# Two row tiles of 64 rows for the attention scores and their maxima, on alternate half steps

## Chip, cores and metric

The program runs on one core of one Trainium2 chip. The metric is the device time of one execution in microseconds. Three timed runs of the kernel before gave 635.09 us as their median (633.9 to 636.69).

## What is computed

Two transformer layers over x of shape 4 x 256 x 512, each with attention and feed-forward side by side on the same layer norm. All matrix products are in float32.

```
xn = layernorm(x)
x  = x + attn0(xn) + (gelu(xn @ W1 + b1) @ W2 + b2)             # W1: 512 x 2048
xn = layernorm(x)
x  = x + attn1(xn) + ((silu(g) * u) @ w3.T + b3), g|u = xn @ w12.T + b12
attn: 32 query heads, 8 key/value heads, head size 16, 256 tokens
      softmax(q @ k.T * scale) @ v, then an output projection
attn1 also has rotary positions and a causal mask
```

## The kernel before

**Precision.** A float32 operand is kept as a rounded part and a remainder, and a product of two operands is three products of parts. In the large projections these are three matmuls (`three`, the helper of line 693). For the scores the three products are stacked in the contraction instead: 16 head dimensions in four groups of rows of `q_sb` and `k_sb` (high, low, high, low; 64 rows), 32 rows of zeros up to `ROWS = 96`, and row 96 (`MROW`), which holds minus the row maxima in `q_sb` and ones in `k_sb`.

**Units.** There are 8 (layer, batch entry) pairs `n`, and each is worked in 4 units of 8 query heads, so 32 units `u` (`LU = 16` per layer). A unit has these steps, each with its own line on TensorE:

- `("m", u, i)`, i = 0 to 7, line 748: query-major scores of two heads, two matmuls of 256 keys (128 where the causal mask allows no more) into one PSUM bank, and in layer 1 a third one, line 753, that adds the causal mask from a bf16 tile. VectorE (line 1067) reduces the bank to minus the maximum of each row.
- `("mt", u)`, line 761: those 16 columns of maxima are transposed, and `mrow` sends them by DMA to row 96 of `q_sb`.
- `("st", u, i)`, i = 0 to 7, lines 778 and 781: key-major scores with the maxima already subtracted through row 96, one matmul of 512 columns (256 where masked) into bank 0 or 1. ScalarE (line 917) takes the exponential into `probs`; in layer 1 GpSimd (line 649) clears the upper triangle.
- `("pv", u, t)`, t = 0, 1, line 800: probabilities times values. Four matmuls stand in four column groups of 32 of the array (each is two instructions, float32 in two passes); then `norm` on VectorE and `ctx` on ScalarE and GpSimd.

**Order.** All engines walk one list, `program_order()`. `unit_slots(u)` makes 8 slots. Slot i has `st` of unit u and one `m` of unit u + 1 (i < 4) or u + 2. `spread` fills each slot with steps of the projections (`up`, `down`, `qkv`, `wo`, in parts of three or six matmuls, line 693) by the table `COST`. `with_followers` appends what drains them: `add` (VectorE, line 1105) one slot after a `down`, `hidden` (ScalarE, lines 936 and 937) right behind `up`. `work_banks` deals the banks `WORK_BANKS = (2, 3, 4, 5, 7)` to everything but `st` and `pv`, the least recently used free one first; the `m` steps take their turn there.

**Waits of `st` and `m`.** `st` number k waits for the exponential k - 2 (two banks in turn). `m` waits for whoever had its bank. The queries of a unit come over `q_parts` in DRAM by two DMAs (line 556), keys over `k_parts` (line 565) into one `k_sb`, whose halves are refilled once the last unit that reads them is through. GpSimd zeroes the spare rows at the start (lines 604 to 612).

## Time and profile before

| | |
|---|---|
| median of 3 runs | 635.09 us |
| the profiled execution | 634.52 us, its span 632.8 us |
| TensorE matmuls (PE) | 586.8 us busy, 93% of the span, 3360 instructions |
| TensorE weight loads (PEld) | 452.0 us, 71%, beside the matmuls |
| VectorE (DVE) | 438.4 us, 69% |
| ScalarE (ACT) | 356.3 us, 56% |
| GpSimd (POOL) | 213.8 us, 34% |
| granted TensorE clock, mean | 0.985 of full speed |

A matmul's record begins with its stream (or with its weight load, where that is not hidden) and ends when a model says that the result is out, so records of back-to-back matmuls overlap. What a matmul costs in a dense stretch is the distance between two starts. Where a row has several matmuls, its length is the distance from the first to the last start and the length of one.

### The profile page before, as it was taken

What the parts mean: (1) busy time and instruction counts of PE and PEld (TensorE: products, weight loads), DVE (VectorE), ACT (ScalarE), POOL (GpSimd) and SP (SyncE); (2) the same over time, 40 slices, a digit from 0 to 9 for tenths busy, and PEclk for the clock granted to TensorE, in tenths of its full rate; (3) what the DMA queues carried; (4) which work ended last, traced back from release to release, by engine and by line L of the source; (5) the groups of instructions that cost most, each with busy time, mean ns of one, the idle gap of its engine ahead of it and who ended that gap; (6) DMA issues with size and microseconds to landing.
All of it is one profiled execution on the core that took longest, in us unless ns stands there. A gap on an engine that the chain in (4) does not pass through costs nothing.

```text
span 632.8 us, 10359 instructions
## 1 busy us (share of the span) xinstructions
PE 586.8 (93%) x3360; PEld 452.0 (71%) x3360; DVE 438.4 (69%) x815; ACT 356.3 (56%) x611; POOL 213.8 (34%) x332
## 2 busy tenths in 40 slices
PE   3788899999999999999999999897999999899985
PEld 2677677787777787677877767666777877667754
DVE  6559967656566576486897685867796887487552
ACT  2337766754564683666585564655655564474440
POOL 5703423122303331111322122443643455254231
PEclk9989999999999999999999999999899999999989
DMA  5574541353233334324543323244433353344001
GB/s 187 173 207 151 134 118 67 102 150 101 69 82 103 99 101 118 84 67 134 151 134 100 85 68 117 84 105 114 127 92 102 84 142 110 85 121 116 2 17 51
DMA packets 29805, 67.30 MB, mean 106 GB/s; under 512 B 4788, under 2 KB 17588, under 8 KB 27704
## 3 DMA queue, kind: packets, MB, share of 16 engines
q1 hardware_dynamic: 21112, 38.32, 22.2%
q0 software_dynamic: 8640, 28.32, 15.2%
q8 instruction: 28, 0.46, 0.3%
q14 instruction: 25, 0.20, 0.1%
HBM read 51.67 MB, written 14.68 MB: 105 GB/s over the span
## 4 chain that ended last, share of the span: by engine, by line
PE 74%; ACT 6%; DVE 6%; DMA 5%; issue 5%; POOL 2%; SPq 1%; ACTq 0%; DVEq 0%; POOLq 0%
PE banks L693 48%; PE banks L748 8%; PE banks L800 7%; PE banks L778 7%; PE banks L753 2%; DMA q_sb<-q_parts 2%; DMA raw<-in_attn 1%; PE banks L781 1%; PE banks L713 1%; ACT L917 1%; ACT probs L917 1%; ACT hid_f L937 1%; ACT L936 1%; POOL probs L649 1%; DMA q_sb<-max_t 1%
## 5 line engine op out<-in xcount | busy, mean ns | idle before, releaser
L1067 DVE TENSOR_REDUCE neg_max<-banks 128x2 f32<-128x512 f32 (+1 forms) x256 | 158.1, 620 | 150.4 <-PE banks L748 93.7
L917 ACT ACTIVATE probs<-banks 128x512 f32<-128x512 f32 (+1 forms) x256 | 137.8, 545 | 193.8 <-PE banks L778 145.6
L693 PE MATMUL banks<-xnT,w_up 128*128 128x512 f32 x576 | 157.4, 407 | 5.4 <-issue 3.7
L693 PE MATMUL banks<-w_down,hid 128*128 128x512 f32 x480 | 129.4, 403 | 4.2 <-ACT hid_f L937 2.0
L693 PEld LDWEIGHTS banks<-xnT,w_up 128*128 128x128 f32 x576 | 102.9, 192 | 33.4 <-issue 13.9
L748 PEld LDWEIGHTS banks<-k_sb,q_sb 96*128 96x128 f32 x512 | 93.6, 193 | 22.7 <-issue 5.6
L693 PEld LDWEIGHTS banks<-w_down,hid 128*128 128x128 f32 x480 | 87.0, 191 | 31.8 <-DVE neg_max L1067 6.7
L748 PE MATMUL banks<-k_sb,q_sb 96*128 96x256 f32 (+1 forms) x512 | 100.3, 278 | 4.8 <-DMA q_sb<-q_parts 4.2
L649 POOL TENSOR_SCALAR_AFFINE_SELECT probs<-probs 128x256 f32<-128x256 f32 x128 | 57.6, 450 | 111.5 <-ACT probs L917 106.6
L778 PE MATMUL banks<-q_sb,k_sb 97*128 97x512 f32 x192 | 79.3, 413 | 11.7 <-ACT probs L917 11.1
L693 PE MATMUL banks<-xnT,w_qkv 128*128 128x256 f32 x576 | 83.7, 293 | 2.3 <-DVE xnT L1011 1.4
L693 PEld LDWEIGHTS banks<-xnT,w_qkv 128*128 128x128 f32 x576 | 77.1, 198 | 5.0 <-DVE xnT L1011 1.8
L1105 DVE TENSOR_TENSOR x_res<-x_res,banks 128x512 f32<-128x512 f32 x96 | 63.8, 678 | 11.2 <-PE banks L693 11.0
L800 PE MATMUL banks<-probs,v_sb 128*32 128x512 f32 (+1 forms) x512 | 61.8, 554 | 1.2 <-POOL probs L649 1.2
L592 POOL DMA_DIRECT2D raw<-in_down x40 | 22.4, 559 | 110.7 <-DVE w_down L973 79.2
L639 POOL TENSOR_TENSOR w_up<-raw,w_up 128x512 fp32r<-128x512 f32 x24 | 32.3, 1348 | 80.4 <-ACT w_up L856 80.1
L778 PEld LDWEIGHTS banks<-q_sb,k_sb 97*128 97x128 f32 x192 | 36.5, 190 | 27.9 <-ACT probs L917 21.2
L693 PE MATMUL banks<-w_out,ctxT 128*128 128x512 f32 x192 | 50.8, 404 | 0.0
L592 POOL DMA_DIRECT2D raw<-in_up x48 | 26.9, 561 | 42.9 <-DVE w_qkv L973 18.3
L693 PEld LDWEIGHTS banks<-w_out,ctxT 128*128 128x128 f32 x192 | 34.4, 190 | 9.2 <-issue 2.9
L917 ACT ACT_TABLE_LOAD x29 | 37.2, 1283 | 0.5
L753 PE MATMUL banks<-mask_qk,identb 128*128 128x256 bf16 x128 | 36.7, 287 | 0.0
(78 smaller groups left out, 629.3 us busy)
## 6 DMA issues: line engine op xcount, KB each, us to landing
q_sb<-q_parts SPq DMA_DIRECT2D x64, 256.0 KB, 4.7
raw<-in_up POOLq DMA_DIRECT2D x48, 256.0 KB, 3.0
raw<-in_down POOLq DMA_DIRECT2D x40, 256.0 KB, 3.0
q_parts<-stage SPq DMA_DIRECT2D x32, 256.0 KB, 2.6
raw<-in_attn POOLq DMA_DIRECT2D x20, 256.0 KB, 3.1
k_parts<-stage SPq DMA_DIRECT2D x16, 256.0 KB, 2.5
k_sb<-k_parts SPq DMA_DIRECT2D x16, 256.0 KB, 4.2
x_res<-in_x SPq DMA_DIRECT2D x4, 512.0 KB, 4.1
```

The lines of the kernel that those rows point to most:

```text
L592: pool.dma_start(raw[:, k % RAW, :], src).then_inc(raw_loaded[k % RAW], 16)
L639: nc.gpsimd.tensor_tensor(to[1], raw[:, k % RAW, :], to[0].bitcast(F32), ALU.subtract).then_inc(lo_split_pool, 1)
L649: nc.gpsimd.affine_select(out=tri, in_=tri, compare_op=ALU.is_ge, fill=0.0, base=0, pattern=[[0, 2], [1, P]], channel_multiplier=-1).then_ ...
L693: mm = nc.tensor.matmul(out_ap, lhs(a), rhs(b_), start=first and j == 0, stop=stop and j == 2, **kw)
L713: mm = nc.tensor.transpose(banks[:, k, c * P:c * P + P], xn[:, t, c * P:c * P + P], ident[:, :])
L748: mm = nc.tensor.matmul(banks[:, k, r * T:r * T + w], q_sb[0:ROWS, u % RING, 2 * g + r, t * P:t * P + P], k_sb[0:ROWS, 4 * f + g, 0:w], st ...
L753: mm = nc.tensor.matmul(diagonal, identb[:, :], mask_qk[:, None, :].to_broadcast([P, 2, P]), start=False, stop=True, skip_group_check=True)
L778: mm = nc.tensor.matmul(bank, keys, q_sb[0:MROW + 1, u % RING, 2 * g:2 * g + 2, :], start=True, stop=True)
L800: mm = nc.tensor.matmul(o, v_sb[:, t, 4 * f + g, :], p_, start=t == 0, stop=t == 1, skip_group_check=True)
L917: nc.scalar.activation(probs[:, i, 0:w], banks[:, ST_BANKS[k % 2], 0:w], ACT.Exp, scale=SCALES[n // B]).then_inc(exp_done, 1)
L1067: nc.vector.tensor_reduce(neg_max[:, s, 2 * g:2 * g + 2, t], banks[:, bank_of[x], :].rearrange("p (r t) -> p r t", r=2)[:, :, 0:w], AX.X, ...
L1105: nc.vector.tensor_tensor(x_res[:, tile, :], x_res[:, tile, :], banks[:, bank_of[y], :], ALU.add).then_inc(wk_emptied, 1)
```

## The change

`m` and `st` become `STEPS = 4` steps per unit of four heads each. `q_sb` and `k_sb` hold half of the heads in rows 0 to 47 and the other half in rows 64 to 111 (`HALF = 64`); three groups of 16 rows carry the three products, and rows 48 and 112 the maxima and ones. Nothing is padded with zeros any more, so the five memsets go. A step's matmuls come in pairs, one on rows 0 to 63 of the array into one bank, one on rows 64 to 127 into another. `m` has its own banks 2 and 3, `st` has 0 and 1, both refilled only when emptied; three banks are left for the rest. One VectorE reduction and one exponential cover both banks of a step.

`st` opens the even slots and `m` the odd ones. `pv` stands right behind the `st` of slots 0 and 4 (before: behind the `m` of slots 1 and 5). In layer 1 the mask matmuls of an `m` step, still of 128 rows, come first and open the banks; the four row-tiled ones follow. The addition of a `down` follows the next costed step instead of coming a slot later, and the triangle on GpSimd (`tri`) a slot after its `st`. `k_sb` has two buffers, loaded once per `n`. Queries and keys now take four DMAs per load, the maxima two. `COST` and `norm`'s slots are changed too.

```diff
-ROWS = 96
-MROW = 96
+HALF = 64
+ROWS = 48
+MROW = 48
+SOON = -1
+STEPS = 4
...
 ST_BANKS = (0, 1)
-WORK_BANKS = (2, 3, 4, 5, 7)
+MAX_BANKS = (2, 3)
+WORK_BANKS = (4, 5, 7)
...
+    if x[0] == "m":
+        return 1 if x[1] < LU else 2
     return {"up": 4, "down": 2, "wo": 4, "qkv": 8}.get(x[0], 1)
...
 def cost(x):
+    if x[0] == "part" and x[1][0] == "m":
+        return 300
     return COST.get((x[1] if x[0] == "part" else x)[0], 0)
...
     if x[0] == "down":
-        return [(1, ("add",) + x[1:])]
+        return [(SOON, ("add",) + x[1:])]
     if x[0] == "split":
         return [(1, ("low", x))]
+    if x[0] == "st" and x[1] >= LU:
+        return [(1, ("tri",) + x[1:])]
...
     for g, slot in enumerate(slots):
-        head = [k for k, x in enumerate(slot) if x[0] in ("st", "m")]
+        head = [k for k, x in enumerate(slot) if x[0] in ("st", "m", "pv")]
...
+            if cost(x):
+                o += soon
+                soon = []
...
-    slots = [[("st", u, i)] for i in range(8)]
-    for i in range(8):
-        if i < 4 and u + 1 < UNITS:
-            slots[i].append(("m", u + 1, i + 4))
-        if i >= 4 and u + 2 < UNITS:
-            slots[i].append(("m", u + 2, i - 4))
+    slots = [[] for _ in range(8)]
+    for j in range(STEPS):
+        w, i = (u + 1, j + 2) if j < 2 else (u + 2, j - 2)
+        maxima = parts(("m", w, i)) if w < UNITS else []
+        slots[2 * j].append(("st", u, j))
+        slots[2 * j + 1] += maxima
+    if u > 0:
+        slots[0].append(("pv", u - 1, 1))
+    slots[4].append(("pv", u, 0))
     if s == 2 and n + 1 < 2 * B:
-        slots[0].append(("load_k", n + 1, 0))
-    if s == 0 and n > 0:
-        slots[0].append(("load_k", n, 1))
+        slots[0].append(("load_k", n + 1))
     if 0 < u < UNITS - 2:
...
-        slots[1].append(("pv", u - 1, 1))
-        slots[2].append(("norm", u - 1, 0))
-        slots[3] += [("norm", u - 1, 1), ("norm", u - 1, 2)]
-        slots[4].append(("norm", u - 1, 3))
...
+        slots[3].append(("norm", u - 1, 3))
+        slots[4].append(("ctx", u - 1))
     if u + 1 < UNITS:
         slots[5] += [("mt", u + 1), ("mrow", u + 1)]
-    slots[5].append(("pv", u, 0))
     if s == 0 and n > 0:
...
-        if (x in wk or x[0] == "up") and x not in bank:
+        if x[0] == "m" and x not in bank:
+            bank[x] = ST_BANKS if x[1] == 0 and x[2] % 2 else MAX_BANKS
+            before[x] = user.get(bank[x])
+            user[bank[x]] = x
+        elif (x in wk or x[0] == "up") and x not in bank:
...
-        if y:
+        if y and y[0] != "m":
...
+        q_sb = sb("q_sb", [P, RING, UH // 2, T], F32R)
+        k_sb = sb("k_sb", [P, 2, NKV // 2, T], F32R)
         v_t = sb("v_t", [P, 2, T])
         v_sb = sb("v_sb", [P, TT, NKV, 2 * HD])
...
+                    rows = qscr[n, s].rearrange("h (e a d c) t -> a (h e) d (c t)", e=2, a=2, c=4)
+                    for a in range(2):
+                        to = q_sb[HALF * a:HALF * a + ROWS, u % RING, :, :].rearrange("p c t -> p (c t)").bitcast(F32)
+                        sp_.dma_start(to[0:2 * HD], rows[a]).then_inc(q_loaded[u % RING], 16)
+                        sp_.dma_start(to[2 * HD:], rows[a, 0:2]).then_inc(q_loaded[u % RING], 16)
...
-                    t, g = divmod(i, 4)
-                    k = work(x)
...
-                    w = T if n < B or t == 1 else P
-                    for r in range(2):
-                        mm = nc.tensor.matmul(banks[:, k, r * T:r * T + w],
-                                              q_sb[0:ROWS, u % RING, 2 * g + r, t * P:t * P + P], k_sb[0:ROWS, 4 * f + g, 0:w],
-                                              start=r == 0, stop=n < B and r == 1, skip_group_check=True)
-                    if n >= B:
-                        diagonal = banks[:, k, :].rearrange("p (r t) -> p r t", r=2)[:, :, t * P:t * P + P]
-                        mm = nc.tensor.matmul(diagonal, identb[:, :], mask_qk[:, None, :].to_broadcast([P, 2, P]),
-                                              start=False, stop=True, skip_group_check=True)
-                    mm.then_inc(wk_filled, 1)
+                    t, pair = divmod(j, 2)
+                    ks = work(x) if opens else bank_of[x]
+                    if opens and not closes:
+                        if x == ("m", LU, 0):
+                            pe.wait_ge(identb_made, 1)
+                        for k in ks:
+                            diagonal = banks[:, k, :].rearrange("p (r t) -> p r t", r=2)[:, :, t * P:t * P + P]
+                            nc.tensor.matmul(diagonal, identb[:, :], mask_qk[:, None, :].to_broadcast([P, 2, P]),
+                                             start=True, stop=False, skip_group_check=True)
+                    if closes:
+                        if j == 0:
+                            pe.wait_ge(q_loaded[u % RING], 64 * (u // RING + 1))
+                            pe.wait_ge(k_loaded[n % 2], 64 * (n // 2 + 1))
+                        w = T if n < B or t == 1 else P
+                        for r in range(2):
+                            for a in range(2):
+                                rows = slice(HALF * a, HALF * a + ROWS)
+                                mm = nc.tensor.matmul(banks[:, ks[a], r * T:r * T + w],
+                                                      q_sb[rows, u % RING, 2 * pair + r, t * P:t * P + P],
+                                                      k_sb[rows, n % 2, 2 * f + pair, 0:w],
+                                                      start=opens and r == 0, stop=r == 1, skip_group_check=True)
+                        mm.then_inc(wk_filled, 1)
...
+                    t, pair = divmod(j, 2)
+                    k = st_index(u, j)
+                    if k:
+                        pe.wait_ge(exp_done, k)
...
+                    q0 = 0 if n < B or t == 0 else P
+                    for a in range(2):
+                        rows = slice(HALF * a, HALF * a + MROW + 1)
+                        mm = nc.tensor.matmul(banks[:, ST_BANKS[a], 0:2 * (T - q0)].rearrange("p (r t) -> p r t", r=2),
+                                              k_sb[rows, n % 2, 2 * f + pair, t * P:t * P + P],
+                                              q_sb[rows, u % RING, 2 * pair:2 * pair + 2, q0:], start=True, stop=True)
                     mm.then_inc(st_filled, 1)
...
                     w = 2 * P if n >= B and t == 1 else 512
-                    nc.scalar.activation(probs[:, i, 0:w], banks[:, ST_BANKS[k % 2], 0:w], ACT.Exp,
+                    nc.scalar.activation(probs[:, 2 * j:2 * j + 2, 0:w], banks[:, 0:2, 0:w], ACT.Exp,
                                          scale=SCALES[n // B]).then_inc(exp_done, 1)
...
-                    nc.vector.tensor_reduce(neg_max[:, s, 2 * g:2 * g + 2, t],
-                                            banks[:, bank_of[x], :].rearrange("p (r t) -> p r t", r=2)[:, :, 0:w],
+                    nc.vector.tensor_reduce(neg_max[:, s, :, pair, :, t],
+                                            banks[:, bank_of[x][0]:bank_of[x][1] + 1, :].rearrange("p a (r t) -> p a r t", r=2)[:, :, :, 0:w],
                                             AX.X, ALU.max, negate=True).then_inc(wk_emptied, 1)
```

What this does to TensorE's queue, first in layer 0, in a unit with both kinds of projection. In these rows L778 and its new line L803 are `st`, L748 and L777 are `m`, L761 and L787 `mt`, L800 and L824 `pv`, L693 and L716 the projections. Before:

```order
L693 MATMUL banks<-xnT,w_up 128x512 x12
L778 MATMUL banks<-q_sb,k_sb 128x512
L748 MATMUL banks<-k_sb,q_sb 128x256 x2
L761 MATMUL banks<-ident,neg_max 16x128
L800 MATMUL banks<-probs,v_sb 32x512 x4
L693 MATMUL banks<-w_down,hid 128x512 x6
L778 MATMUL banks<-q_sb,k_sb 128x512
L748 MATMUL banks<-k_sb,q_sb 128x256 x2
L693 MATMUL banks<-w_down,hid 128x512 x9
```

And now:

```order
L716 MATMUL banks<-xnT,w_up 128x512 x12
L803 MATMUL banks<-q_sb,k_sb 128x512 x2
L824 MATMUL banks<-probs,v_sb 32x512 x4
L716 MATMUL banks<-xnT,w_up 128x512 x9
L777 MATMUL banks<-k_sb,q_sb 128x256 x4
L787 MATMUL banks<-ident,neg_max 16x128
L716 MATMUL banks<-xnT,w_up 128x512 x3
L716 MATMUL banks<-w_down,hid 128x512 x6
L803 MATMUL banks<-q_sb,k_sb 128x512 x2
L716 MATMUL banks<-w_down,hid 128x512 x9
```

Each `st` is two matmuls and each `m` four, with projections between them; `pv` follows `st`.

In layer 1, where L753 and L767 are the masks. Before:

```order
L693 MATMUL banks<-xnT,w_up 128x512 x6
L778 MATMUL banks<-q_sb,k_sb 128x512
L748 MATMUL banks<-k_sb,q_sb 128x256 x2
L753 MATMUL banks<-mask_qk,identb 128x2x128
L800 MATMUL banks<-probs,v_sb 32x2x128 x4
L778 MATMUL banks<-q_sb,k_sb 128x512
L748 MATMUL banks<-k_sb,q_sb 128x256 x2
L753 MATMUL banks<-mask_qk,identb 128x2x128
```

And now:

```order
L803 MATMUL banks<-q_sb,k_sb 128x512 x2
L824 MATMUL banks<-probs,v_sb 32x2x128 x4
L767 MATMUL banks<-mask_qk,identb 128x2x128 x2
L777 MATMUL banks<-k_sb,q_sb 128x256 x4
L716 MATMUL banks<-w_out,ctxT 128x512 x6
L803 MATMUL banks<-q_sb,k_sb 128x512 x2
L716 MATMUL banks<-w_out,ctxT 128x512 x6
L767 MATMUL banks<-mask_qk,identb 128x2x128 x2
L777 MATMUL banks<-k_sb,q_sb 128x256 x4
```

The two mask matmuls stand ahead of the four of the maxima; `st` stands apart, with `pv` behind it.

## Rows read from the trace of the kernel before

**Rows 1.** The page, parts 1 (busy time) and 4 (the chain that ended last).

```profile
PE 586.8 (93%) x3360; PEld 452.0 (71%) x3360; DVE 438.4 (69%) x815; ACT 356.3 (56%) x611; POOL 213.8 (34%) x332
...
PE 74%; ACT 6%; DVE 6%; DMA 5%; issue 5%; POOL 2%; SPq 1%; ACTq 0%; DVEq 0%; POOLq 0%
```

**Rows 2.** Busy time by stretch: PE, PEld, DVE, ACT, POOL, clock, DMA share, GB/s.

```profile
100.00:200.00 100.00, 98.26 (x538) 75.74 (x537) 62.74 (x110) 58.23 (x95) 27.81 (x33) 1.00 0.33 91
...
300.00:400.00 100.00, 97.96 (x556) 75.11 (x549) 76.57 (x140) 60.93 (x102) 25.47 (x38) 1.00 0.36 104
```

**Rows 3.** Timeline of PE in layer 0: start us, us, engine, line, op, count [idle].

```profile
199.94 0.40 PE L748 MATMUL banks<-k_sb,q_sb 96*128 96x256 f32 x2
200.27 1.06 PE L800 MATMUL banks<-probs,v_sb 128*32 128x512 f32 x8
201.27 0.96 PE L693 MATMUL banks<-xnT,w_up 128*128 128x512 f32 x3
...
202.30 0.40 PE L748 MATMUL banks<-k_sb,q_sb 96*128 96x256 f32 x2
202.54 2.23 PE L693 MATMUL banks<-xnT,w_up 128*128 128x512 f32 x9
204.61 0.40 PE L778 MATMUL banks<-q_sb,k_sb 97*128 97x512 f32 x1
```

**Rows 4.** The same view at 200.95, the second four of `pv`.

```profile
200.73 0.61 PE L800 MATMUL banks<-probs,v_sb 128*32 128x512 f32 x4
```

**Rows 5.** Timeline of the weight loads in that place.

```profile
200.27 0.16 PEld L800 LDWEIGHTS banks<-probs,v_sb 128*32 128x32 f32 x8
201.27 0.53 PEld L693 LDWEIGHTS banks<-xnT,w_up 128*128 128x128 f32 x3 [0.84 <-issue]
```

**Rows 6.** PE around an `mt`.

```profile
43.74 0.27 PE L761 MATMUL banks<-ident,neg_max 128*16 128x128 f32 x1
...
44.09 0.40 PE L693 MATMUL banks<-xnT,w_up 128*128 128x512 f32 x1
```

**Rows 7.** Weight loads around it.

```profile
43.51 0.09 PEld L761 LDWEIGHTS banks<-ident,neg_max 128*16 128x16 f32 x1
43.74 0.30 PEld L748 LDWEIGHTS banks<-k_sb,q_sb 96*128 96x128 f32 x2
```

**Rows 8.** PE in layer 1, a step of 128 keys with its mask.

```profile
383.28 0.34 PE L748 MATMUL banks<-k_sb,q_sb 96*128 96x128 f32 x2
...
383.50 0.94 PE L693 MATMUL banks<-w_down,hid 128*128 128x512 f32 x3
```

**Rows 9.** PE in layer 1, a step of 256 keys with its mask.

```profile
485.48 0.40 PE L748 MATMUL banks<-k_sb,q_sb 96*128 96x256 f32 x2
...
485.76 0.70 PE L693 MATMUL banks<-xnT,w_up 128*128 128x512 f32 x2
```

**Rows 10.** Who PE waited for: us in total, times, longest us.

```profile
PE banks L778 <- ACT probs L917: 11.1, 7, 3.6
```

**Rows 11.** Groups of instructions: count | busy us, mean ns | idle before, releasers.

```profile
L1067 DVE TENSOR_REDUCE neg_max<-banks 128x2 f32<-128x512 f32 x192 | 131.4, 687 | 119.5 <-PE banks L748 93.7 <-PE banks L753 24.7
...
L917 ACT ACTIVATE probs<-banks 128x512 f32<-128x512 f32 x192 | 114.3, 599 | 146.3 <-PE banks L778 145.6
...
L1105 DVE TENSOR_TENSOR x_res<-x_res,banks 128x512 f32<-128x512 f32 x96 | 63.8, 678 | 11.2 <-PE banks L693 11.0
...
L1067 DVE TENSOR_REDUCE neg_max<-banks 128x2 f32<-128x256 f32 x64 | 26.7, 418 | 30.9 <-PE banks L753 30.6
...
L917 ACT ACTIVATE probs<-banks 128x256 f32<-128x256 f32 x64 | 24.0, 384 | 47.5 <-PE banks L781 47.4
...
L612 POOL MEMSET q_sb<- 32x2048 f32 x3 | 5.5, 1818 | 0.0
```

**Rows 12.** The first `m` on PE.

```profile
35.74 0.48 PE L748 MATMUL banks<-k_sb,q_sb 96*128 96x256 f32 x2 [1.90 <-DMA q_sb<-q_parts]
```

**Rows 13.** The DMA queue ahead of that `m`.

```profile
29.81 1.73 SPq L556 DMA_DIRECT2D q_sb<-q_parts  x4
```

More of the change, by code:

```diff
@@ L118, in with_followers @@
                     o.append(y)
+                elif d == SOON:
+                    soon.append(y)
                 else:
                     due[g + d].append(y)
-    for left in due[len(slots):]:
+    for left in due[len(slots):] + [soon]:
         o += left
@@ L138, in start_slots @@
     o += [parts(("up", 0, 0, 0)) + [("load_q", 2), ("load_bias",)]]
-    ms = spread([[("m", 0, i)] for i in range(8)], parts(("qkv", 1, 2)), [1] * 8)
+    ms = spread([[("m", 0, j)] for j in range(STEPS)], parts(("qkv", 1, 2)), [1] * STEPS)
     later = parts(("up", 0, 1, 0)) + parts(("qkv", 1, 0)) + [("bias",)]
-    ms += spread([[("m", 1, i)] for i in range(4)], later, [1] * 4)
-    ms[8] += [("mt", 0), ("mrow", 0)]
-    ms[9] += split(0, "up", 2, 3)
-    ms[10] += split(0, "down", 0, 1)
+    ms += spread([[("m", 1, 0)], [("m", 1, 1)], [], []], later, [1] * 4)
+    ms[4] += [("mt", 0), ("mrow", 0)]
+    ms[5] += split(0, "up", 2, 3)
+    ms[6] += split(0, "down", 0, 1)
     return o + ms
@@ L327, in build @@
     stg = numbered(order, "store")
+    stores = [2 if x[2] < 2 else 1 for x in order if x[0] == "store"]
     stt = numbered(order, "stats")
@@ L468, in wait_low_part, with wait_stored @@
                 eng.wait_ge(lo_split_pool, lo_pool[x] + 1)
+        def wait_stored(eng, k):
+            eng.wait_ge(staged[k % 2], 16 * sum(stores[i] for i in range(k % 2, k + 1, 2)))
         def wait_tile_sum(eng, x):
@@ L532, in _ @@
                         sp_.dma_start(bias_raw[row:row + 2, :, :], out_b).then_inc(bias_loaded, 16)
+                    sp_.wait_ge(made, ONES)
+                    for row in (MROW, HALF + MROW):
+                        sp_.dma_start(k_sb[row:row + 1, :, :, :].rearrange("o a c t -> o (a c t)").bitcast(F32),
+                                      ones[0:2 * NKV // 2 * T // P, :].bitcast(F32)).then_inc(ones_loaded, 16)
                 if x[0] == "store":
@@ L603, in _ @@
             load(3)
[L604 to L613 removed]
+            for k in range(4, EARLY):
+                load(k)
             nc.gpsimd.memset(v_sb[:, :, :, :], 1.0).then_inc(made, 1)
@@ new lines, in _ @@
+                    if closes:
[4 more added lines that the diff above has]
+                        for r in range(2):
+                            for a in range(2):
+                                rows = slice(HALF * a, HALF * a + ROWS)
[4 more added lines that the diff above has]
+                        mm.then_inc(wk_filled, 1)
@@ L776, in _ @@
-                    bank = banks[:, bank_k, :].rearrange("p (r t) -> p r t", r=2)
-                    if n < B or t == 0:
-                        mm = nc.tensor.matmul(bank, keys, q_sb[0:MROW + 1, u % RING, 2 * g:2 * g + 2, :], start=True, stop=True)
-                    else:
-                        later = banks[:, bank_k, 0:2 * P].rearrange("p (r t) -> p r t", r=2)
-                        mm = nc.tensor.matmul(later, keys, q_sb[0:MROW + 1, u % RING, 2 * g:2 * g + 2, P:], start=True, stop=True)
+                    t, pair = divmod(j, 2)
@@ L1059, in _ @@
                 if x[0] == "m":
-                    _, u, i = x
+                    _, u, j = x
                     n, s, f = unit(u)
-                    t, g = divmod(i, 4)
+                    t, pair = divmod(j, 2)
                     dve.wait_ge(wk_filled, wk[x] + 1)
@@ L1133, in _layouts @@
 def _layouts(i):
+    rows = [(8 * e + d, a, c) for e in range(2) for a in range(2) for d in range(8) for c in range(4)]
     def q_rows(head_row):
-        return np.array([head_row(_PERM_HEAD[s][h]) + d for s in range(S) for d in range(HD) for h in range(UH)])
+        return np.array([head_row(_PERM_HEAD[s][2 * (2 * (c // 2) + a) + c % 2]) + d for s in range(S) for d, a, c in rows])
     def kd(base):
-        return np.array([base(g) + d for d in range(HD) for g in range(NKV)])
+        return np.array([base(2 * c + a) + d for d, a, c in rows])
     def gd(base):
@@ L1166, in _layouts @@
     cos, sin = np.cos(ang), np.sin(ang)
-    row = np.arange(P) // 8
+    row = np.array([d for d, _, _ in rows])
     rope = np.stack([cos[row % 8], np.where((row < 8)[:, None], sin[row % 8], -sin[row % 8])], 1).astype(np.float32)
```

143 lines of the change are left out of this document (58 added, 85 removed).

## The prediction

> **What bounds the kernel now.** I read the page first. TensorE is busy for 93% of the span and holds 74% of the chain that ended last [rows 1]. Next, the busy time by stretch: between 100 and 400 us TensorE is busy for 98 of each 100 us at full clock, while VectorE has 63 to 77 and ScalarE 58 to 61 [rows 2]. A matmul's record is longer than its place in the queue, so the timeline must say whether such a stretch is dense. It is: the nine `up` matmuls at 202.54 have (2.23 - 0.40) / 8 = 0.23 us from start to start, and `st` follows at 204.61, which is 9 x 0.23 later [rows 3]. So in a dense stretch a matmul of 512 columns costs 0.23 us, one of 256 costs 0.12 (`m` at 202.30, two matmuls, the next work at 202.54), and weight loads are hidden. What is added to TensorE's queue there is added to the time; what VectorE or ScalarE save is not.
>
> **What a change of tile costs, as far as this trace has it.** The only tiled matmuls are those of `pv`. The `m` matmuls ahead of it start at 199.94 and 200.06, so the queue would be free at 200.18; `pv` starts at 200.27: 0.09 us of waiting. Its second four start at 200.73, 0.46 after the first, and the next `up` only at 201.27, 0.54 later: again 0.08 to 0.09 of waiting [rows 3, 4]. The first weight load of that `up` starts at 201.27 too, where elsewhere it starts during the matmul ahead [rows 5]; from its three matmuls (last start 201.27 + 0.96 - 0.40 = 201.83) the true first stream began at 201.83 - 2 x 0.23 = 201.37, so the load cost 0.10 in the open. Going into a tile or out of it is thus 0.09 of waiting, and the first full-width weight load, 0.10, is uncovered. I take 0.19 per switch, 0.38 for a visit.
>
> The same rows show that tiles run together: four instructions start at once [rows 4]. I take it that two row tiles do so too, that their two weight loads run together, and that the second pair's loads hide behind the first pair.
>
> The Trainium skill ("TensorEngine Tiling (Array Packing)", Tiling Modes) says that changing the tiling mode, not just the tile, drains TensorE. By that rule each of the new visits pays; the `pv` rows agree, and the `mt` rows below look as if they don't. Its section on restrictions excludes column tiling for float32 transposes, which would explain `mt`; no row here shows which.
>
> **The terms on TensorE.**
>
> - `m` on 256 keys: 64 steps in layer 0 and 32 in layer 1. Before, two old steps: 2 x 2 x 0.12 = 0.48. Now 0.38 + two pairs of 0.12 = 0.62. In layer 1 a mask costs the same 0.12 as before and stands next to the old `m` and ahead of the new one: from 485.48 to the true start of the next work (485.76 + 0.70 - 0.39 - 0.23 = 485.84) are 0.36, less 0.24 for the two matmuls [rows 9]. 96 x 0.14 = +13.4 us.
> - `m` on 128 keys: 32 steps. Before, one old step takes 0.31 with its mask (383.50 + 0.94 - 0.39 - 2 x 0.23 = 383.59, from 383.28) [rows 8], so two take 0.62. Now two masks 0.24, the visit 0.38, the first pair covering the next load 0.10, the second pair 0.06: 0.78. 32 x 0.16 = +5.1.
> - `mt` follows 32 of the `m` steps. Its load has 16 columns (a record of 0.09 [rows 7]) and the load behind it is hidden, so 0.09 of the open 0.10 falls away: 32 x -0.09 = -2.9.
> - `st` of 512 columns, 96 steps: before 0.46. Alone (49) it is 0.38 + 0.23 = 0.61; with `pv` behind it (47) the way out is the way into `pv`, which was paid before too: 0.19 + 0.23 = 0.42. 49 x 0.15 - 47 x 0.04 = +5.5.
> - `st` of 256 columns, 32 steps, half of them with `pv`: before 0.24, now 0.50 or 0.31. 16 x 0.26 + 16 x 0.07 = +5.3.
>
> Sum +26.4 us. The concurrency that the change buys is smaller than the switches that it adds: 128 visits for `m` and 65 for `st` alone.
>
> **The rest.** VectorE: 687 ns for 512 columns and 418 for 256 [rows 11] are 1.05 ns a column and 149 ns fixed; 128 reductions fewer save 19 us. ScalarE the same way: 599 and 384 ns, 169 fixed, 22 us saved. Both lie beside TensorE, so I cost them at nothing. If TensorE's queue shrank instead, they would have to be looked at again.
>
> `st` had two banks in turn and waited for the exponential two steps back, 5 us; now it waits for the last one, but the steps are 5 us apart. The 11.1 us lost there now [rows 10] I leave as they are; it could be 5 us less or more.
>
> Banks: the projections share three, where with `m` they had five. Counting along the order, some 10 groups (first `down` of a unit, `xn`, `mt`) now take a bank whose user closed only 0.7 us earlier, and must wait for an addition of 0.68 [rows 11] or for a copy. 10 x 0.5 = +5; the bounds are 0 and 14 (some 20 more are two steps away).
>
> Start: the first `m` waits for the queries at 35.74 [rows 12], sent by four DMA issues in 1.73 us [rows 13]; now eight go out, but the first unit's four are followed at once, so +0.9. The five memsets of 1.8 us [rows 11] are gone, but the chain to this `m` goes by DMA, so nothing.
>
> 26.4 + 5 + 0.9 = 32 us on the profiled execution's own 634.5 us gives 666.5; the median stands 0.6 above it. I say 666. With the bounds of the terms this case reaches from 650 to 690.
>
> **Rivals.**
>
> - **The row switch is free (faster).** `mt` uses 16 columns of the array and shows no wait: it starts at 43.74, `m` behind it loads at 43.74, and two `m` matmuls later the next work starts at 44.09 = 43.74 + 0.11 + 2 x 0.12 [rows 6, 7]. If only column groups in use, or `pv`'s two-pass float32, cause the wait, the visits cost nothing: `m` 96 x -0.24 and 32 x -0.22, `st` 96 x -0.23 and 32 x -0.12, together -56 us. With 5 us of bank waits and 1 of start that is 585; since TensorE then leaves less cover, I say 590, in a range of 578 to 606. It decides as soon as a switch costs under about 0.10 us.
> - **Half of the price (mostly faster).** A row tile keeps the columns' wiring, so perhaps only one side waits, or the load is covered on one. 193 visits less 0.19 each are -37 us: 629, range 613 to 649.
> - **The tiles don't run together (slower still).** Matmuls of the two tiles in turn add 96 x 0.24 + 32 x 0.28 for `m` and 96 x 0.23 + 32 x 0.12 for `st`: +58 us, 724. If only their weight loads go in turn, it is about 0.2 per `m` and 0.1 per `st`, 128 of each: +38, 704. The four starts of `pv` within one row speak against it, but those tiles are columns. By the skill ("TensorE: Matmul & The Clock Gate", Part 3) a pack of row tiles takes one matmul and about 4 ns more for each further tile, which would exclude this case.
>
> **Chances.** Forecast 0.46. Free switch 0.19, half price 0.23, no concurrency 0.12. The `pv` rows are the nearest to what is added, and constant, hence the lead; rows and columns need not behave alike, hence the rest. The range leaves out the last rival and the lower half of the free one: 590 to 690. A change of under 0.5% (3.2 us) can't be told from none here. Faster by more: 0.19 + 0.17 of the half price = 0.36; within: 0.05; slower: 0.59. The forecast's own range is 650 to 690.
>
> **What would show it.** In the timeline of the changed kernel, after an `m` or `st` the next projection's weight load starts together with its matmul, 0.09 us after the stream's end, and the true start is 0.10 later; the two matmuls of a pair start within 10 ns. A step of `m` on 256 keys takes about 0.6 us of queue, a lone `st` also 0.6. TensorE stays the bound at 98% in the middle of the run. I am wrong if the projection's load begins during the row-tiled matmul, if the second tile starts 0.1 or 0.2 us after the first, or if the added time lies in waits for ScalarE, VectorE or banks.

## Result: 700 us, 10% slower, beyond the forecast's range

The changed kernel takes 699.91 us in the median of four runs (699.08 to 700.78), the kernel before 634.50 beside it: a ratio of 1.103, 95% interval 1.099 to 1.107. The direction was right; the size was not: 65 us more, where the sum had 32 and the range ended at 690. The profiled execution took 700.78 us, its span is 699.1 (632.8 before). Of the runs below one, of the first experiment (678.79 us), fell in a slower state of the chip; without it that kernel's median is 673.65 instead of 674.67.

Page of the changed kernel, parts 1, 2 (TensorE's clock in 40 slices) and 4:

```profile
PE 627.4 (90%) x3360; PEld 399.1 (57%) x3360; DVE 438.7 (63%) x687; ACT 340.6 (49%) x483; POOL 193.1 (28%) x263
...
PEclk9859998999999999999999999997899999989999
...
PE 72%; DVE 8%; DMA 7%; issue 5%; ACT 3%; SPq 2%; POOL 2%; DVEq 0%; ACTq 0%; POOLq 0%
```

Beside [rows 1]: TensorE is still what the chain is made of, but its share of the span fell from 93% to 90% and that of the chain from 74% to 72%, while VectorE rose from 6% to 8% and DMA from 5% to 7%. So the added time isn't TensorE's queue alone. There are also slices with a 5, a 7 or an 8 in the clock row; the mean granted clock is 0.951, and it was 0.985 before.

**The tiles do what the forecast said.** TensorE around one `m` (L777) on 256 keys, from the timeline; then the weight loads there; then TensorE between 170.25 and 170.30:

```profile
170.22 0.50 PE L777 MATMUL banks<-k_sb,q_sb 48*128 48x256 f32 x4
170.65 0.51 PE L716 MATMUL banks<-xnT,w_qkv 128*128 128x256 f32 x2
```

```profile
170.22 0.30 PEld L777 LDWEIGHTS banks<-k_sb,q_sb 48*128 48x128 f32 x4
170.65 0.41 PEld L716 LDWEIGHTS banks<-xnT,w_qkv 128*128 128x128 f32 x3
```

```profile
170.01 0.28 PE L716 MATMUL banks<-xnT,w_qkv 128*128 128x256 f32 x1
170.22 0.39 PE L777 MATMUL banks<-k_sb,q_sb 48*128 48x256 f32 x2
```

The last projection ahead starts at 170.01 and streams 256 columns, 0.12 us: the queue is free at 170.13, and `m` starts 0.09 later. The next projection's matmul and its weight load both start at 170.65; its second matmul starts at 170.65 + 0.51 - 0.28 = 170.88, so the first true stream is at 170.76. Visit: 170.76 - 170.13 = 0.63 us, forecast 0.62. The third fence is the view of 170.25 to 170.30 alone: two `m` matmuls are running there, so the second had started by 170.30, where in turn it would be 0.12 behind the first, at 170.34. The matmuls of a pair run together. The same place for `st` (L803) with `pv` behind it, weight loads:

```profile
235.82 0.19 PEld L803 LDWEIGHTS banks<-q_sb,k_sb 49*128 49x128 f32 x2 [0.36 <-issue]
```

Two weight loads in 0.19 us, and the page has 188 ns as the mean of one. So they run together, and the rival in which they go in turn, which gave 704 us, is excluded, close as its number is. The free switch and the half price are excluded by the same rows.

**What was not foreseen: waits.** The waits of TensorE in the changed kernel (us in total, times, longest):

```profile
PE banks L777 <- DMA q_sb<-q_parts: 23.5, 3, 13.3
PE banks L736 <- DVE xn L1029: 8.1, 1, 8.1
PE banks L716 <- DVE xnT L1035: 7.5, 5, 2.1
PE banks L803 <- ACT probs L941: 6.7, 6, 3.1
PE banks L736 <- DVE x_res L1129: 5.1, 3, 1.7
PE banks L716 <- DVE max_t L1099: 3.0, 3, 1.8
```

All rows of this view add up to 67.7 us, before to 40.4. `m` waited for the queries for 4.2 us in all before, now for 23.5 in three waits; the second row was there before (9.6). The three rows that name `xnT`, `x_res` and `max_t` are new or larger: there a matmul or a transpose waits until VectorE has emptied a bank.

The three waits for the queries are 13.35 us at the start, 5.37 ahead of 481.72 and 4.8 near 617. The slowest landing is behind the second one. The chain of waits there (start us, us, what), in the changed kernel:

```profile
467.80 0.63 SPq L594
...
468.53 0.62 SPq L583
469.19 0.62 SPq L584
469.85 0.62 SPq L583
470.52 11.15 DMA q_sb<-q_parts
481.67 0.04 issue
481.72 0.69 PE banks L777 x3
```

A load of queries that landed 5.31 us after its issue in the kernel before ("30.19 5.31 DMA q_sb<-q_parts" in the same view, for the first unit) takes 11.15 here. At the start it is another transfer that is late. The chain there, then the first `m`:

```profile
22.87 9.33 DMA q_parts<-stage
...
34.24 5.82 DMA q_sb<-q_parts
```

```profile
40.10 0.80 PE L777 MATMUL banks<-k_sb,q_sb 48*128 48x256 f32 x4 [13.35 <-DMA q_sb<-q_parts]
```

The load itself takes 5.82 us, but the store of the queries ahead of it (`q_parts<-stage`), issued behind four key loads of the new shape, takes 9.33. It took 4.07 before and takes 4.68 in the first experiment below, where the key loads have another shape. What the DMA engines do around the second wait, by stretch (PE, PEld, DVE, ACT, POOL, clock, DMA share, GB/s):

```profile
470.60:474.00 3.40, 3.40 (x21) 2.48 (x19) 3.33 (x7) 1.34 (x2) 0.90 (x1) 1.00 0.26 100
474.00:477.00 3.00, 2.34 (x18) 0.95 (x17) 1.47 (x3) 1.73 (x4) 1.21 (x2) 1.00 0.16 64
...
479.40:493.00 13.60, 10.21 (x47) 6.97 (x47) 6.91 (x12) 5.00 (x9) 3.13 (x6) 0.50 0.19 59
```

```profile
31.00:35.50 4.50, 2.84 (x7) 1.66 (x5) 0.00 (x0) 0.00 (x0) 0.91 (x2) 0.70 0.95 228
```

The second fence is the kernel before while its queries are on the way: 0.95 of 16 DMA engines are busy and move 228 GB/s. Now it is 0.26 of 16, that is 4.2 engines with 100 GB/s, then 2.5 engines with 64, about 25 GB/s for each. The loads changed shape: the source pattern of one is now `(h e) d (c t)`, with 4 or 2 in the outer place, where it was a list of full rows. If a load of 128 KB goes by 4 engines and one of 64 KB by 2, both put 32 KB on each engine that they use. Eight of them follow each other here (four of keys, four of queries), 256 KB if two engines are common to all; at 25 GB/s that is some 10 us, an estimate from these rows. From the first of the eight issues (465.75) to the landing at 481.67 are 15.9 us, so the estimate covers two thirds of it.

The Trainium skill ("DMA: Bandwidth & Descriptors", the section on why a DMA increments its semaphore by 16) says that a DMA runs on the largest number of engines up to 16 that divides the slowest dimension of both its sides, and that the queues of SP and ScalarE take the lowest-numbered ones. That rule gives 4 and 2 engines here and the rows agree with it.

From 479.4, still in the wait, the clock is at 0.50, TensorE's lower level, 1.2 GHz, for 13.6 us, as the third line has it. Before the change such stretches were 17 us of the execution, in five pieces of 3.4; now they are 68 us, half of it around the two longest waits for the queries (20.4 us from 28.8, 13.6 from 479.4).

### The profile page after: what moved, and what is told of

Read it like the earlier page. It is cut to its first block, busy times and chain, and to the rows that moved or that the text cites. A ratio compares the mean times of both kernels' runs of the same rounds, so it can differ in the third digit from the quotient of the medians.

```text
span 699.1 us, 9832 instructions
## 1 busy us (share of the span) xinstructions
PE 627.4 (90%) x3360; PEld 399.1 (57%) x3360; DVE 438.7 (63%) x687; ACT 340.6 (49%) x483; POOL 193.1 (28%) x263
## 4 chain that ended last, share of the span: by engine, by line
PE 72%; DVE 8%; DMA 7%; issue 5%; ACT 3%; SPq 2%; POOL 2%; DVEq 0%; ACTq 0%; POOLq 0%
PE banks L716 48%; PE banks L824 7%; PE banks L777 7%; PE banks L803 6%; DMA q_sb<-q_parts 4%; DVE hid L1150 2%; PE banks L767 2%; DVE x_res L1129 1%; DMA q_parts<-stage 1%; PE banks L736 1%; DVE neg_max L1091 1%; DMA raw<-in_attn 1%; PE banks L787 1%; DMA q_sb<-max_t 1%; POOL probs L672 1%
## 5 line engine op out<-in xcount | busy, mean ns | idle before, releaser
L1091 DVE TENSOR_REDUCE neg_max<-banks 128x4 f32<-128x1024 f32 (+1 forms) x128 | 139.5, 1090 | 156.5 <-PE banks L777 156.0
L941 ACT ACTIVATE probs<-banks 128x1024 f32<-128x1024 f32 (+1 forms) x128 | 117.6, 919 | 198.5 <-PE banks L803 198.2
L716 PE MATMUL banks<-xnT,w_up 128*128 128x512 f32 x576 | 162.6, 415 | 0.1
L716 PE MATMUL banks<-w_down,hid 128*128 128x512 f32 x480 | 137.8, 421 | 11.9 <-DVE xnT L1035 4.6
L716 PEld LDWEIGHTS banks<-xnT,w_up 128*128 128x128 f32 x576 | 101.2, 190 | 41.0 <-issue 10.6
L716 PEld LDWEIGHTS banks<-w_down,hid 128*128 128x128 f32 x480 | 89.5, 197 | 49.7 <-issue 15.5
L716 PE MATMUL banks<-xnT,w_qkv 128*128 128x256 f32 x576 | 91.2, 311 | 3.7 <-DVE xnT L1035 2.8
L716 PEld LDWEIGHTS banks<-xnT,w_qkv 128*128 128x128 f32 x576 | 80.9, 210 | 12.1 <-DVE xnT L1035 3.5
L777 PE MATMUL banks<-k_sb,q_sb 48*128 48x256 f32 (+1 forms) x512 | 64.5, 332 | 25.3 <-DMA q_sb<-q_parts 23.5
L777 PEld LDWEIGHTS banks<-k_sb,q_sb 48*128 48x128 f32 x512 | 39.8, 192 | 60.3 <-issue 30.4
L803 PE MATMUL banks<-q_sb,k_sb 49*128 49x512 f32 (+1 forms) x256 | 61.8, 479 | 7.9 <-ACT probs L941 6.7
L824 PE MATMUL banks<-probs,v_sb 128*32 128x512 f32 (+1 forms) x512 | 62.4, 560 | 2.5 <-POOL probs L672 2.4
L680 POOL TENSOR_TENSOR ctxT<-o_t,ctxT 128x256 fp32r<-128x256 f32 x32 | 23.5, 735 | 128.4 <-ACT ctxT L949 128.4
L672 POOL TENSOR_SCALAR_AFFINE_SELECT probs<-probs 128x512 f32<-128x512 f32 x64 | 45.8, 716 | 45.1 <-ACT probs L941 40.4
L716 PE MATMUL banks<-w_out,ctxT 128*128 128x512 f32 x192 | 52.6, 411 | 0.0
L803 PEld LDWEIGHTS banks<-q_sb,k_sb 49*128 49x128 f32 x256 | 24.5, 188 | 48.7 <-issue 36.5
L716 PEld LDWEIGHTS banks<-w_out,ctxT 128*128 128x128 f32 x192 | 33.8, 188 | 16.6 <-issue 8.0
L1150 DVE TENSOR_TENSOR hid<-hid_f,hid 128x512 fp32r<-128x512 f32 x40 | 37.2, 930 | 1.9 <-ACT hid_f L961 1.9
```

Of the source, the lines that this page charges most:

```text
L672: nc.gpsimd.affine_select(out=tri, in_=tri, compare_op=ALU.is_ge, fill=0.0, base=0, pattern=[[0, 2], [0, 2], [1, P]], channel_multiplier=- ...
L680: nc.gpsimd.tensor_tensor(ctxT[:, 1, s, :], o_t[:, :], ctxT[:, 0, s, :].bitcast(F32), ALU.subtract).then_inc(ctx_lo, 1)
L716: mm = nc.tensor.matmul(out_ap, lhs(a), rhs(b_), start=first and j == 0, stop=stop and j == 2, **kw)
L777: mm = nc.tensor.matmul(banks[:, ks[a], r * T:r * T + w], q_sb[rows, u % RING, 2 * pair + r, t * P:t * P + P], k_sb[rows, n % 2, 2 * f + p ...
L803: mm = nc.tensor.matmul(banks[:, ST_BANKS[a], 0:2 * (T - q0)].rearrange("p (r t) -> p r t", r=2), k_sb[rows, n % 2, 2 * f + pair, t * P:t ...
L824: mm = nc.tensor.matmul(o, v_sb[:, t, 4 * f + g, :], p_, start=t == 0, stop=t == 1, skip_group_check=True)
```

## The experiments

The chip's own time of the kernel before is 634.1 (634.0 in the last group). Unless said otherwise an edit is made to the changed kernel.

**1. The loads, and the stretches.** Two suspects, alone and together. First the rows of a tile in an order that makes each load a plain list of rows:

```diff
-                    rows = qscr[n, s].rearrange("h (e a d c) t -> a (h e) d (c t)", e=2, a=2, c=4)
+                    rows = qscr[n, s].rearrange("h (e d a c) t -> a (h e d) (c t)", e=2, a=2, c=4)
...
-    rows = [(8 * e + d, a, c) for e in range(2) for a in range(2) for d in range(8) for c in range(4)]
+    rows = [(8 * e + d, a, c) for e in range(2) for d in range(8) for a in range(2) for c in range(4)]
```

The keys' pattern is changed in the same way, and `rows[a, 0:2]` becomes `rows[a, 0:HD]`.

> Changed kernel, but the rows of queries and keys are ordered so that each load is one run of rows at one distance (32 or 16 rows of 4 KB) instead of blocks of 4 or 2 by 8. Same bytes, same number of DMAs, same result. Theory A (part of the excess over the forecast is the slow landing of these loads, 13.4 us of waiting at the start and 5.4 and 4.9 us later, and the half clock that follows such waits): landing falls from 8 to 11 us to about 5, the first m starts near 33 us, and the time falls by 20 to 30 us to 670 to 680. Theory B (the loads are not what holds the queue up; banks and tile switches do): the waits move to the next late thing and the time stays above 692.

Measured: 674.67 us, ratio 1.063 [1.053, 1.073], 25.2 less than the changed kernel. Its page, part 6 (KB each, us to landing), and what is left of the wait:

```profile
q_sb<-q_parts SPq DMA_DIRECT2D x64, 128.0 KB, 3.0
q_sb<-q_parts SPq DMA_DIRECT2D x64, 64.0 KB, 3.2
```

```profile
PE banks L777 <- DMA q_sb<-q_parts: 5.3, 1, 5.3
```

The wait is 18 us shorter, all waits together are 21.7 shorter (67.7 to 46.0), and the mean clock rises from 0.951 to 0.969. The first `m` starts at 32.05 instead of 40.10. So the order of rows inside a tile, which changes no arithmetic, is worth about 25 of the 65 us. The runs of this kernel spread from 668 to 679 us, so a difference with it is good to some 6 us.

Next, `m` moved back into one stretch with `st`, with the slow loads:

```diff
-        slots[2 * j].append(("st", u, j))
-        slots[2 * j + 1] += maxima
+        slots[2 * j] += maxima + [("st", u, j)]
```

> Changed kernel, but m stands in the same slot as st, right ahead of it, so that m, st and (in two slots of four) pv make one stretch of tiled matmuls. 128 visits to the row tile fall away. Theory A (a visit costs 0.38 us of TensorE's queue, and the queue is the bound): -49 us at most, the loads half a step tighter and still slow, so 650 to 660. Theory B (the alternation of the two is worth something, since each has one pair of banks): under 20 us are gained, the rest comes back as waits of m or st for VectorE or ScalarE.

Measured: 682.34, ratio 1.080 [1.071, 1.088], only 17.6 less. `m` stands half a step earlier, so the slow loads have less time:

```profile
PE banks L776 <- DMA q_sb<-q_parts: 29.7, 5, 11.2
PE banks L776 <- issue: 14.1, 8, 5.3
```

Two rows of 44 us against 24.4 (23.5 + 0.9) before the edit. The second row names no releaser; with quick loads, in the next experiment, it is 0.8 us, so it belongs to the loads too. The gain is in the range of Theory B, but what comes back is waits for DMAs, not for VectorE or ScalarE. Then both edits:

> Both edits together. Theory A: they add up, 620 to 632, at or below the kernel before, which is PE-bound by its untiled st and m. Theory B: no lower than 645.

Measured: 628.21, ratio 0.991 [0.986, 0.995]: 0.9% below the kernel before, a small difference but clear of the noise. One stretch saves 46.5 us against the first experiment, where 128 visits for `m` fall away. That would be 0.36 each (forecast 0.38), but the clock rose as well, from 0.969 to 0.986; without its share an estimate, worked out behind the experiments, leaves 0.32. The price of one visit is read from the timeline:

```profile
152.66 0.39 PE L715 MATMUL banks<-w_out,ctxT 128*128 128x512 f32 x1
152.98 0.50 PE L776 MATMUL banks<-k_sb,q_sb 48*128 48x256 f32 x4
153.32 0.39 PE L802 MATMUL banks<-q_sb,k_sb 49*128 49x512 f32 x2
153.64 0.50 PE L715 MATMUL banks<-w_out,ctxT 128*128 128x512 f32 x1
```

`st` starts 0.34 after `m`: two pairs of 0.12 and the uncovered weight load, 0.10; there is no second wait of 0.09 between two steps in the same tiles. From the end of the `w_out` stream ahead (152.66 + 0.23 = 152.89) to the first full-width stream behind (153.64 + 0.10) are 0.85 us for `m` and `st` together, 0.38 more than their streams of 0.24 and 0.23: one visit where there were two.

**2. The tiles themselves.** The first experiment with `m` and `st` over all rows, 0 to 112, rows 32 to 63 set to zero once at the start:

```diff
-                                rows = slice(HALF * a, HALF * a + ROWS)
+                                rows = slice(0, HALF + ROWS)
...
-                        rows = slice(HALF * a, HALF * a + MROW + 1)
+                        rows = slice(0, HALF + MROW + 1)
```

> The kernel of e1 with the same order of work, banks, loads and waits, but every m and st matmul contracts rows 0 to 111 (or 112) at once, so that no row tile is used and the matmuls of a pair run in turn. It computes both heads' products added together, which is not the reference's result; VectorE fills rows 32 to 63 with zeros once at the start. Theory A (tiles cost 26 us more in switches than they save): 26 us less than e1, so about 648. Theory B (the tiles save time on the whole and the schedule around them costs more than the excess): slower than e1.

Measured: 659.97, ratio 1.044 [1.037, 1.052]. The waits hold one that the edit made itself, of 13.5 us, for the row of ones behind the first keys. So once more, with that DMA ahead of the first keys:

```diff
+                    if n == 0:
+                        sp_.wait_ge(spare, 2)
+                        sp_.wait_ge(made, ONES)
+                        for row in (MROW, HALF + MROW):
+                            sp_.dma_start(k_sb[row:row + 1, :, :, :].rearrange("o a c t -> o (a c t)").bitcast(F32),
```

> e4 again (untiled matmuls in the order of e1), but the ones rows are filled ahead of the first keys, because in e4 the first m stood 13.5 us for them, which belongs to the edit and not to the question. Theory A (tile switches cost 26 us more than tiles save, less the overlap with other waits): 648 to 655, so 20 to 26 us below e1's 675. Theory B (e4's 660 was right and the tiles cost only 15 us net): within 3 us of 660.

Measured: 654.71, ratio 1.034 [1.028, 1.040]: 20.0 us less than with tiles. And TensorE's waits in this run add up to 57.9 us against 46.0 with them, 11.9 more: part of what leaves the queue comes back as waiting for others. Some 4 us of it are the edit's own, at the start (`xn` 10.2 against 8.0, the first queries 6.9 against 5.3).

**3. The banks.** One bank taken from the projections of the kernel before, which has no row tiles:

```diff
-WORK_BANKS = (2, 3, 4, 5, 7)
+WORK_BANKS = (2, 3, 4, 5)
```

> The kernel before with one work bank less (2, 3, 4, 5 without 7), shared by m and the projections as before. Measures the price of banks alone, where the change leaves three to the projections and two to m. Theory A (banks are worth some 10 to 15 us in the changed kernel): 5 to 12 us slower than before. Theory B (the order of additions and reductions is what makes those waits, not the number of banks): no measurable difference.

Measured: 651.53, ratio 1.030 [1.025, 1.035]: one bank is 17.4 us, more than either theory had, in a kernel in which nothing else changed. TensorE's waits rise from 40.4 to 53.2, and the mean clock stays (0.985, now 0.984). The changed kernel has three for the projections. The place where such a wait arises, in the changed kernel, TensorE and then VectorE:

```profile
114.11 0.50 PE L777 MATMUL banks<-k_sb,q_sb 48*128 48x256 f32 x4 [0.85 <-issue]
114.54 0.28 PE L787 MATMUL banks<-ident,neg_max 128*16 128x128 f32 x1
116.53 0.66 PE L736 MATMUL banks<-ident,xn 128*128 128x128 f32 x4 [1.71 <-DVE x_res L1129]
119.12 0.79 PE L716 MATMUL banks<-w_down,hid 128*128 128x512 f32 x1 [1.94 <-DVE xnT L1035]
```

```profile
114.65 1.22 DVE L1091 TENSOR_REDUCE neg_max<-banks 128x4 f32<-128x1024 f32 x1 [3.47 <-PE banks L777]
115.79 0.68 DVE L1129 TENSOR_TENSOR x_res<-x_res,banks 128x512 f32<-128x512 f32 x1
116.39 2.08 DVE L1150 TENSOR_TENSOR hid<-hid_f,hid 128x512 fp32r<-128x512 f32 x1
118.39 0.68 DVE L1035 TENSOR_TENSOR xnT<-banks,xnT 128x512 fp32r<-128x512 f32 x1
```

The addition that empties a bank takes 0.68 us, as forecast, but it stands behind the reduction of 1.22, which is now of both tiles at once. The next copy stands behind a `hid` of 2.08. TensorE waits 1.71 and 1.94 us, not the 0.5 that the forecast put down. VectorE isn't short of time here: it stood idle for 3.47 us until `m` had filled its banks, and the addition stood behind that reduction in its list.

Then all banks of `m` and the projections in one pool of five (2 to 6, with `pv` in 7), where `m` takes the neighbouring pair that was used longest ago, on top of the first experiment:

```diff
-MAX_BANKS = (2, 3)
-WORK_BANKS = (4, 5, 7)
-PV_BANK = 6
+WORK_BANKS = (2, 3, 4, 5, 6)
+PV_BANK = 7
...
+            free = [k for k in recent if k not in taken]
+            pairs = [(k, k + 1) for k in free if k + 1 in free]
+            free = min(pairs, key=lambda p: max(recent.index(k) for k in p))
```

> e1 (two stretches, quick loads), but m takes two neighbouring free banks out of a pool of five that it shares with the projections, as before, instead of owning two (pv moves to bank 7). Theory A (in e1 some 20 us of waiting at xn, w_down and the masks come from three banks): 8 to 15 us faster than e1's 675. Theory B (they come from VectorE being late whatever the banks): within 3 us of e1.

Measured: 651.84, ratio 1.031 [1.025, 1.036], 22.8 less than the first experiment, more than either theory had. The waits fell by 11.0 (46.0 to 35.0): those for `xnT` and `x_res` are 1.6 us, where they were 15.8, those for `neg_max` 8.7, where they were 2.8. The mean clock rose from 0.969 to 0.986; the stretches at half clock are 42 us without the pool and 18 with it. That fewer waits are the reason is argued, not shown by a run. Both together are what the banks were worth here.

**4. Does the order inside a stretch matter?** `st` ahead of `m` instead of behind it, the masks still first:

```diff
-        slots[2 * j] += maxima + [("st", u, j)]
+        slots[2 * j] += maxima[:-1] + [("st", u, j)] + maxima[-1:]
```

> e3 with st ahead of m inside the stretch (in layer 1 the masks first, then st, then m, then pv). The m of e3 waited 7.4 us for VectorE's last reduction ahead of its masks. Theory A (that wait is only a matter of being 0.3 us later, the masks still wait): within 4 us of e3's 628. Theory B (the reduction is just late): 4 to 8 us faster than e3.

Measured: 627.74, ratio 0.992 [0.989, 0.994]: the same as the third. The order inside costs nothing, as Theory A had it.

With the pool as well:

> All three repairs: quick loads, one stretch (masks, st, m, pv) and the pool of five banks of e8. Theory A (loads, banks and visits are separate prices): e7's 628 less the 15 to 23 us that the pool was worth in e8, so 605 to 613, clearly faster than the kernel before. Theory B (with fewer visits TensorE has less to cover, and VectorE's and ScalarE's lateness takes most of it back): 618 or more.

Measured: 629.70, ratio 0.992 [0.989, 0.995], no gain. The expected 15 to 23 us stayed out. In one stretch `m` shares its banks with steps that stand near it, and where it waits the stretch breaks in two. Timeline:

```profile
165.48 0.50 PE L810 MATMUL banks<-q_sb,k_sb 49*128 49x512 f32 x2
167.63 0.50 PE L784 MATMUL banks<-k_sb,q_sb 48*128 48x256 f32 x4 [1.65 <-ACT hid_f L968]
```

`m` waits 6.1 us in all for `hid_f` in the pool. But all waits together fell, from 52.8 us to 47.0, and the mean clock is 0.970 where it was 0.986: by the traces it is the clock that takes the gain back. Why it is lower here stays open, since without tiles (below) `m` waits 6.0 us for `hid_f` and the clock is 0.987.

**5. The tiles again, with enough banks.** The pooled kernels, each without tiles (the same edit as in 2):

> e8 without row tiles: every m and st matmul contracts rows 0 to 111 or 112 at once (not the reference's result). Two stretches, with banks and loads mended, so little slack is left for the switches to hide in. Theory A (two visits per half step cost 26 us more of TensorE's queue than tiles save; in e1 against e5 20 us were seen): 20 to 27 us below e8, so 625 to 632. Theory B (part of those 20 us was bank waiting): 15 us or less below e8.

Measured: 639.11, ratio 1.008 [1.005, 1.011]. In two stretches the tiles cost 12.7 us net, the range of Theory B; its reason is taken up below.

> e9 without row tiles, in the same way (not the reference's result). Theory A (in one stretch a visit of 0.38 us, half of it paid by pv anyway in two slots of four, buys 0.47 us of concurrency): the tiles are worth 10 to 16 us here, so this is that much slower than e9. Theory B (they never pay): the same as e9 or faster.

Measured: 637.53, ratio 1.006 [1.003, 1.009]. In one stretch they gain 7.8 net, less than the 10 to 16 expected. Without tiles the move to one stretch is worth only 1.6 us (639.11 to 637.53), with them 22.1 (651.84 to 629.70). So the sign of the whole idea hangs on how many visits pay the switch. The first of these kernels, timeline:

```profile
170.84 0.64 PE L790 MATMUL banks<-k_sb,q_sb 112*128 112x256 f32 x4
171.32 0.27 PE L800 MATMUL banks<-ident,neg_max 128*16 128x128 f32 x1
```

Four untiled matmuls take 0.48 us to the next start, with no wait and the weight loads hidden, as the forecast took from [rows 3]. So the difference in the queue is the 0.14 a step that it used. Yet the profiled executions are only 9.2 us apart (649.81 and 640.57; the medians 12.7), because the waits of TensorE rise by 12.4 when the tiles go (35.0 to 47.4; 2.1 of it is `xn` at the start, behind the zeroing that the edit adds): 9.2 + 12.4 = 21.6, beside 26.4 in the sum. The waits had risen by as much in the kernel with three banks (11.9), so bank waiting isn't what made 20.0 into 12.7.

## Where the 65 us come from

| step | us | difference |
|---|---|---|
| changed kernel | 699.91 | |
| loads as plain rows | 674.67 | 25.2 |
| five pooled banks | 651.84 | 22.8 |
| no tiles | 639.11 | 12.7 |
| kernel before | 634.04 | 5.1 |

The order in which the pieces are taken away matters: without tiles in the three-bank kernel they are 20.0, not 12.7. The two largest pieces can't be ranked, since both are taken from the first experiment with its spread of some 6 us.

The traces split the time in another way. The table has the span of each profiled execution, TensorE's waits, and, as an estimate of what the lower clock cost, half of the time in which matmuls are busy in stretches at 0.50. The rest is the queue itself, with the start and the end.

| profiled execution | span | waits | half clock | rest |
|---|---|---|---|---|
| kernel before | 632.8 | 40.4 | 8.5 | 583.9 |
| changed kernel | 699.1 | 67.7 | 24.7 | 606.7 |
| loads as plain rows | 671.9 | 46.0 | 18.5 | 607.4 |
| the same, pooled banks | 648.1 | 35.0 | 7.4 | 605.7 |
| the same, no tiles | 638.9 | 47.4 | 6.9 | 584.6 |
| plain rows, one stretch | 622.1 | 47.8 | 7.4 | 566.9 |
| the same, `st` first, pooled | 625.5 | 47.0 | 16.9 | 561.6 |
| the same, no tiles | 634.6 | 45.9 | 6.4 | 582.3 |

The change adds 22.8 us to the queue, 27.3 of waits and 16.2 by the clock, 66.3 in all. Loads and banks leave the queue as it is; only tiles and visits change it. The last 5.1 us of the first table lie in waits (47.4 against 40.4): those for `neg_max` are 11.6 against 1.8 and those of `st` for the maxima's DMA 4.8 against 0.5, while those for the exponentials fell. One stretch takes 40.5 us from the queue, 44.1 with the pool: 0.32 to 0.34 for each of the 128 visits, by this coarse estimate, where the timeline above shows 0.38.

## The prediction, step by step

- **What bounds the kernel**: right. The dense stretches are still TensorE's, and what left VectorE's and ScalarE's queues gave nothing. That VectorE would have less to do at all was right for the reductions (139.5 us beside 158.1 in [rows 11]) and wrong for the engine: its busy time is 438.7, as before. `hid` takes 930 ns where it took 727, which is 8 of the 19 us, and `rot_b` takes 1467 where it took 1003, 5.6 more.
- **A switch at 0.19, a visit at 0.38**: right, from the `pv` rows alone. A visit with its streams reads 0.63 against 0.62, and where two become one the timeline has 0.38 less than two. That column tiles and row tiles cost the same was the open choice; it held.
- **The sum of +26.4 on TensorE**: near as time in its queue (22.8 by the second table, 21.6 from tiles against no tiles; which of its terms is too large stays open), too large as time of the kernel: 12.7 to 20.0 net. The step took a longer queue as pure loss, but waits for ScalarE and VectorE hid behind the added switches; the totals of waits show 12 us of that.
- **"10 x 0.5 = +5; the bounds are 0 and 14"** for the banks: wrong; 22.8 measured, and 17.4 for a single bank in the kernel before. The step counted an addition of 0.68 us and not what stands ahead of it in VectorE's list (a reduction of 1.22, a `hid` of 2.08), and it gave the waits no price beyond their length. The sum has no term for the clock at all, and the clock is 16.2 us by the estimate above.
- **"eight go out, but the first unit's four are followed at once, so +0.9"** for the start: wrong; the loads cost 25.2. The step counted issues on SP's queue, of which the rows of before spoke, and took the landing as it was. It did not look at the shape of the new source patterns, though they stand in the diff, not at the store that queues behind the first of these loads (9.33 us instead of 4.07), and not at later units: two of the three waits are not at the start.
- **The exponential's wait left as it is**: near. It was 11.1 and is 6.7, the better end of what was said.
- **The rivals**: tiles run together and the switch isn't free; three fell by the rows shown above. The true case was not among them: a chain from the load's shape to a wait to the clock. Of its own signs of being wrong one came true, added time in waits for banks; waits for DMAs were not on the list. The range should have been wider upward, by a load bound from the shape. The direction rested on the queue above all (26.4 of 32 us), and that held; most of what was measured lies elsewhere, though: 43.5 of 66.3 us are waits and clock.

`mt` behind `m` pays nothing more, as forecast: it starts 0.43 after `m` (114.11 to 114.54 above), which is two pairs of 0.12, the load's 0.10 and the 0.09 of the way out.

## To carry to other kernels

Count a tile's gain in visits, not in matmuls: here a visit costs 0.38 us of TensorE's queue, so tiled steps belong side by side, and the same tiles that cost 13 to 20 us in two stretches gain 8 in one (with the pooled banks; with three banks the one stretch wasn't run without tiles). When an edit changes a layout, read the shape of each load that follows from it, outermost dimension first, before counting anything else. A bank of PSUM given up costs what stands ahead in the emptying engine's list, not only the emptying instruction; test it alone in the old kernel, which takes one line.

The version with both edits (plain rows, `m` and `st` in one stretch) is the best found, with `st` or `m` first: 628 us, 0.9% under the kernel before, interval 0.5% to 1.4%.

## What the runs showed of the hardware

- Loads whose outer dimension is 4 or 2 kept 4.2 and then 2.5 of 16 DMA engines busy, at about 25 GB/s each, and landed after up to 11.15 us; the same bytes as 32 or 16 rows landed in 3.0 and 3.2 (medians). The issue of the plain rows on SP's queue is cheaper too:

```profile
26.88 0.42 SPq L584
27.34 0.42 SPq L583
27.80 4.21 DMA q_sb<-q_parts
```

  (the chain of the first experiment; 0.62 each in the changed kernel).
- Stretches at half clock stand behind waits: 17 us of such stretches before the change, 68 after. Each of them has a wait of TensorE of 1.3 us or more shortly ahead, but not every such wait has a stretch behind it (2.1 us at 404.7 in the kernel before has none). The longest, 20.4 us from 28.8, holds the wait for the first queries:

```profile
28.80:49.20 20.40, 9.10 (x40) 7.43 (x40) 4.90 (x4) 0.00 (x0) 0.00 (x0) 0.50 0.22 77
```

  TensorE is busy for 9.10 us of it. So a wait on the bounding engine can cost more than its length.
- Row tiles of 48 rows and column tiles of 32 columns pay the same wait at a switch, 0.09 us in and 0.09 out. The first weight load of 128 columns behind a switch, 0.10 us, is uncovered: on both sides for the row tiles, on the way out for the column tiles.
